# Last stage: scores computed with tokens as rows, and the compression units of four tiles stacked in column groups

## The reference, cut to what matters

```
cluster_scores = xf @ cluster_sigs.T            # 8 columns
tile_scores    = xf @ sigs.T                    # 64 columns
h    = gelu(xf @ compress_w1 + compress_b1)     # 32 units
comp = tanh(h @ compress_w2 + compress_b2)      # 2 values
```

## Time and profile before

| | |
|---|---|
| median of 3 runs | 1382.83 us (1378.61 to 1390.34) |
| the profiled execution | 1387.69 us, its span 1385.9 us |
| PE busy | 1106.9 us, 80% of the span |
| DVE busy | 1053.8 us, 76% |
| ACT busy | 834.5 us, 60% |
| POOL busy | 593.4 us, 43% |

### The profile page before, as it was taken

How to read it: one execution, slowest core, us unless ns; L and a number is a source line. 1 busy time by engine, 2 the same in 40 slices (tenths; PEclk the granted TensorE clock), 3 DMA queues, 4 the chain that set the end, 5 groups by cost and what they waited for, 6 DMA issues and landing times. The chain is left out here.

```text
span 1385.9 us, 36351 instructions
## 1 busy us (share of the span) xinstructions
PE 1106.9 (80%) x11411; PEld 781.1 (56%) x11411; DVE 1053.8 (76%) x2823; ACT 834.5 (60%) x1904; POOL 593.4 (43%) x696
## 2 busy tenths in 40 slices
PE   2599999999999997514999999999999997601330
PEld 1366666666666664303777777777777774301220
DVE  6478988998988894643777777777777772698885
ACT  1267777777777775362666676666666664401675
POOL 6224444344344432414554545555455505000676
PEclk9789999999999999756999999999999998855555
DMA  1645555555555540305544444444445421100011
GB/s 41 154 107 138 132 128 136 127 129 139 128 134 131 135 111 6 122 8 138 126 114 114 119 117 122 117 107 126 112 121 120 107 53 69 54 0 0 24 46 53
DMA packets 122515, 137.28 MB, mean 99 GB/s; under 512 B 12560, under 2 KB 110160, under 8 KB 113232
## 3 DMA queue, kind: packets, MB, share of 16 engines
q1 hardware_dynamic: 121408, 136.45, 39.7%
q10 hardware_dynamic: 1040, 0.00, 0.0%
HBM read 85.03 MB, written 37.75 MB: 89 GB/s over the span
## 5 line engine op out<-in xcount | busy, mean ns | idle before, releaser
L372 DVE TENSOR_REDUCE attn_negmax<-attn_row_ps 128x2 f32<-128x512 f32 (+1 forms) x1024 | 610.7, 618 | 204.4 <-PE attn_row_ps L554 186.1
L313 ACT ACTIVATE attn_probs<-attn_col_ps 128x512 f32<-128x512 f32 (+1 forms) x1024 | 541.3, 550 | 248.0 <-PE attn_col_ps L576 246.2
L554 PE MATMUL attn_row_ps<-k_st,q_st 72*128 72x256 bf16 (+1 forms) x2048 | 370.8, 263 | 15.7 <-DMA k_st<-attn_scratch 14.0
L576 PE MATMUL attn_col_ps<-q_st,k_st 74*128 74x256 bf16 (+1 forms) x2048 | 370.2, 262 | 1.6 <-ACT attn_probs L313 0.7
L593 PE MATMUL attn_out_ps<-attn_probs,v_sb 128*32 128x256 f32 (+1 forms) x4096 | 242.8, 361 | 0.7 <-ACT attn_probs L313 0.7
L576 PEld LDWEIGHTS attn_col_ps<-q_st,k_st 74*128 74x128 bf16 x2048 | 184.1, 99 | 89.6 <-ACT attn_probs L313 57.2
L554 PEld LDWEIGHTS attn_row_ps<-k_st,q_st 72*128 72x128 bf16 x2048 | 202.1, 99 | 42.2 <-issue 15.5
L593 PEld LDWEIGHTS attn_out_ps<-attn_probs,v_sb 128*32 128x32 f32 x4096 | 109.3, 110 | 90.1 <-issue 29.0
L287 POOL TENSOR_SCALAR attn_var<-attn_mv 128x2 f32<-128x2 f32 x64 | 14.3, 223 | 329.6 <-DVE attn_mv L435 329.6
L550 PE MATMUL attn_row_ps<-mask_qk,ident_h 128*128 128x256 bf16 x512 | 140.8, 275 | 18.0 <-DMA k_st<-attn_scratch 17.5
L572 PE MATMUL attn_col_ps<-mask_kq,ident_h 128*128 128x256 bf16 x512 | 141.5, 276 | 0.6 <-ACT attn_probs L313 0.5
(11 more groups left out here) (230 smaller groups left out, 1707.4 us busy)
## 6 DMA issues: line engine op xcount, KB each, us to landing
q_st<-attn_scratch SPq DMA_DIRECT2D x192, 192.0 KB
k_st<-attn_scratch SPq DMA_DIRECT2D x192, 192.0 KB
attn_scratch<-attn_parts SPq DMA_DIRECT2D x64, 384.0 KB, 2.8
attn_scratch<-attn_parts SPq DMA_DIRECT2D x64, 128.0 KB, 2.8
x_in<-in_L_attn_x_dram SPq DMA_DIRECT2D x32, 128.0 KB, 2.6
x_all<-in_L_attn_x_dram SPq DMA_DIRECT2D x32, 128.0 KB, 6.9
moe_xs<-x_all SPq DMA_DIRECT2D x8, 512.0 KB, 3.5
x_in<-x_mid SPq DMA_DIRECT2D x32, 128.0 KB, 2.5
```

What stands on the lines that cost most here:

```text
L313: nc.scalar.activation(probs_of(st, 3, u)[:, j, 0:W], col_ps[:, n % 2, 0:W], ACT.Exp, scale=scale).then_inc(probs_kept, 1)
L372: nc.vector.tensor_reduce(negmax[:, t, 2 * p:2 * p + 2], row_ps[:, row_bank(st, u), 0:2 * keys].rearrange("p (a k) -> p a k", a=2), AX_X, ...
L554: last = nc.tensor.matmul(bank[:, a * keys:(a + 1) * keys], q_st[0:KROWS, sl, h, t * P:(t + 1) * P], k_st[0:KROWS, sl, h, 0:keys], start=n ...
L576: last = nc.tensor.matmul(bank[:, t * N:(t + 1) * N - first], k_st[0:rows, sl, h, t * P:(t + 1) * P], q_st[0:rows, sl, h, first:N], start= ...
```

## The change

**On PE**, the one product with tokens as columns is replaced by two sets:

- units: four products per group, stationary `compress_w1` (128 x 32), moving the `xT` of tile t (128 columns), each written to rows 32t to 32t+31 of `h_ps`, so in four column groups of the array;
- scores: four products per group, stationary the `xT` of tile t (128 x 128), moving the 72 signature columns. The result has tokens as rows, so the back transposes (L1298, L1300) and the copy to `sT` (L1364) go.

**The second product** becomes one: the stationary is `hT`, now 128 rows (4 tiles x 32 units) by 128 tokens, the moving one a block-diagonal `cw2` (128 x 8). It yields two values for each tile, tokens as rows. The copy to `compT` (L1326) goes. Gelu works on 128 x 128 instead of 32 x 512.

**The pipeline** is one step shorter (depth 4 instead of 5). **The loads**: the bias and `compress_w2` are each loaded four times, once for each block of 32 rows, so that 25 transfers are issued instead of 19.

```diff
-SPLINE_LOADS = 9 + 2 * 5
+SPLINE_LOADS = 7 + 2 * SG + 2 * 5
...
+    for t in range(SG):
+        rows = slice(COMP * t, COMP * (t + 1))
+        eng.dma_start(cb1[rows, :], w["L1_ffn_compress_b1"].rearrange("(n one) -> n one", one=1))\
+            .then_inc(mem["ffn_loaded"], 16)
+        eng.dma_start(cw2[rows, 2 * t:2 * t + 2], w["L1_ffn_compress_w2"]).then_inc(mem["ffn_loaded"], 16)
...
-            pipeline(eng, step, 2, 5, SPLINE_GROUPS, 0)
+            pipeline(eng, step, 2, 4, SPLINE_GROUPS, 0)
...  (PE)
                         wait(pe, h_kept, st.seq(2))
-                        wait(pe, sT_kept, st.seq(2))
-                        nc.tensor.matmul(p_ps[:, j, :], sigs[:, :], xT[:, j, :], start=True, stop=True)\
-                            .then_inc(products_ready, 1)
+                        for t in range(SG):
+                            last = nc.tensor.matmul(h_ps[COMP * t:COMP * (t + 1), j, 0:P], sigs[:, AT_H:P],
+                                                    xT[:, j, t * P:(t + 1) * P], start=True, stop=True,
+                                                    skip_group_check=True)
+                        last.then_inc(h_ready, 1)
+
+                        wait(pe, scores_kept, st.seq(2))
+                        for t in range(SG):
+                            last = nc.tensor.matmul(s_ps[:, j, t * NS:(t + 1) * NS], xT[:, j, t * P:(t + 1) * P],
+                                                    sigs[:, 0:NS], start=True, stop=True)
+                        last.then_inc(scores_ready, 1)
                     if st.has(2):
                         j = st.slot(2)
                         pe.wait_ge(h_kept, st.seq(2, c=1))
-                        wait(pe, compT_kept, st.seq(3))
-                        apart(pe, mem)
-                        for t in range(SG):
-                            last = nc.tensor.matmul(c_ps[32 * t:32 * t + 32, j, 0:P], cw2[AT_H:P, :],
-                                                    hT[AT_H:P, j, t * P:(t + 1) * P], start=True, stop=True,
-                                                    tile_position=(AT_H, 32 * t), skip_group_check=True)
-                        last.then_inc(compT_ready, 1)
-                    if st.has(3):
-                        j = st.slot(3)
-                        pe.wait_ge(sT_kept, st.seq(3, c=1))
-                        pe.wait_ge(compT_kept, st.seq(3, c=1))
-                        wait(pe, scores_kept, st.seq(4, 2))
-                        for t in range(SG):
-                            nc.tensor.transpose(s_ps[:, j, t * NS:(t + 1) * NS], sT[:, j, t * P:(t + 1) * P],
-                                                ident[0:NS, 0:NS])
-                        nc.tensor.transpose(s_ps[:, j, COMP_AT:COMP_AT + P], compT[:, j, :], ident[:, :])\
-                            .then_inc(scores_ready, 1)
+                        wait(pe, hidden_kept, st.seq(3))
+                        nc.tensor.matmul(c_ps[:, j, 0:2 * SG], hT[:, j, :], cw2[:, :], start=True, stop=True)\
+                            .then_inc(hidden_ready, 1)
...  (ACT)
-                        nc.scalar.activation(hT[AT_H:P, j, :], p_ps[AT_H:P, j, :], ACT.Gelu, bias=cb1[AT_H:P, :])\
+                        nc.scalar.activation(hT[:, j, :], h_ps[:, j, 0:P], ACT.Gelu, bias=cb1[:, :])\
...
-                        nc.scalar.copy(compT[:, j, :], c_ps[:, j, 0:P]).then_inc(compT_kept, 1)
...  (DVE)
+                    if st.has(1):
+                        j, tiles = st.slot(1), bass.ds(st.seq(1, SG), SG)
+                        dve.wait_ge(scores_ready, st.seq(1, c=1))
                         nc.vector.tensor_copy(scores[:, tiles, :].rearrange("p t n -> p (t n)"),
+                                              s_ps[:, j, 0:SG * NS]).then_inc(scores_kept, 1)
+                    if st.has(2):
+                        j, tiles = st.slot(2), bass.ds(st.seq(2, SG), SG)
+                        dve.wait_ge(hidden_ready, st.seq(2, c=1))
+                        nc.vector.tensor_copy(comp[:, tiles, :], c_ps[:, j, 0:2 * SG].rearrange(
+                            "p (t m) -> p t m", m=2)).then_inc(hidden_kept, 1)
-                        nc.vector.tensor_copy(sT[:, j, :], p_ps[0:NS, j, :]).then_inc(sT_kept, 1)
```

More of the change, by code:

```diff
@@ L1110, in load_spline @@
                    (sigs[:, AT_H:P], w["L1_ffn_compress_w1"]),
-                   (cb1[AT_H:P, :], w["L1_ffn_compress_b1"].rearrange("(n one) -> n one", one=1)),
-                   (cw2[AT_H:P, 0:2], w["L1_ffn_compress_w2"]),
                    (mem["cb2"][:, :], wide(w["L1_ffn_compress_b2"], 2)),
@@ L1186, in spline_ffn @@
         xT = sb("xT", [P, 2, SG * P])
-        sT = sb("sT", [NS, 2, SG * P])
-        hT = sb("hT", [P, 2, SG * P])
-        compT = sb("compT", [P, 2, P])
+        hT = sb("hT", [P, 2, P])
         scores = sb("scores", [P, TILES, NS])
@@ L1212, in spline_ffn @@
         xs_loaded = [sem(f"xs_loaded{j}") for j in range(2)]
[L1213 to L1216, removed]
+        xT_ready, xT_kept, h_ready, h_kept = (sem(x) for x in ("xT_ready", "xT_kept", "h_ready", "h_kept"))
+        scores_ready, scores_kept, hidden_ready, hidden_kept = (
+            sem(x) for x in ("scores_ready", "scores_kept", "hidden_ready", "hidden_kept"))
         x_beta_kept, mv_cleared = sem("x_beta_kept"), sem("mv_cleared")
@@ L1222, in scored @@
         def scored(eng, step):
-            pipeline(eng, step, 2, 5, SPLINE_GROUPS, 0)
+            pipeline(eng, step, 2, 4, SPLINE_GROUPS, 0)
         with nc.psum_tensor("ffn_t_ps", [P, 2, 512], F32) as t_ps, \
-                nc.psum_tensor("ffn_p_ps", [P, 2, 512], F32) as p_ps, \
+                nc.psum_tensor("ffn_h_ps", [P, 2, 512], F32) as h_ps, \
                 nc.psum_tensor("ffn_c_ps", [P, 2, 512], F32) as c_ps, \
                 nc.psum_tensor("ffn_s_ps", [P, 2, 512], F32) as s_ps, nc.Block() as block:
-            COMP_AT = SG * NS
             @block.sync
@@ L1310, in step @@
                         act.wait_ge(xT_ready, st.seq(0, c=1))
-                        wait(act, products_ready, st.seq(1))
+                        wait(act, scores_ready, st.seq(1))
                         nc.scalar.copy(xT[:, j, :], t_ps[:, j, :]).then_inc(xT_kept, 1)
@@ L1315, in step @@
                         j = st.slot(1)
-                        act.wait_ge(products_ready, st.seq(1, c=1))
-                        wait(act, compT_ready, st.seq(2))
-                        nc.scalar.activation(hT[AT_H:P, j, :], p_ps[AT_H:P, j, :], ACT.Gelu, bias=cb1[AT_H:P, :])\
+                        act.wait_ge(h_ready, st.seq(1, c=1))
+                        wait(act, hidden_ready, st.seq(2))
+                        nc.scalar.activation(hT[:, j, :], h_ps[:, j, 0:P], ACT.Gelu, bias=cb1[:, :])\
                             .then_inc(h_kept, 1)
[L1321 to L1325, removed]
-                        nc.scalar.copy(compT[:, j, :], c_ps[:, j, 0:P]).then_inc(compT_kept, 1)
                 scored(act, step)
@@ L1351, in step @@
                 def step(st):
-                    if st.has(3):
-                        j, tiles = st.slot(3), bass.ds(st.seq(3, SG), SG)
-                        dve.wait_ge(scores_ready, st.seq(3, c=1))
+                    if st.has(1):
+                        j, tiles = st.slot(1), bass.ds(st.seq(1, SG), SG)
+                        dve.wait_ge(scores_ready, st.seq(1, c=1))
                         nc.vector.tensor_copy(scores[:, tiles, :].rearrange("p t n -> p (t n)"),
[L1356 to L1363, removed]
-                        nc.vector.tensor_copy(sT[:, j, :], p_ps[0:NS, j, :]).then_inc(sT_kept, 1)
+                                              s_ps[:, j, 0:SG * NS]).then_inc(scores_kept, 1)
[4 more added lines that the diff above has]
+                            "p (t m) -> p t m", m=2)).then_inc(hidden_kept, 1)
                 scored(dve, step)
-                dve.wait_ge(scores_kept, 2 * SPLINE_GROUPS)
+                dve.wait_ge(scores_kept, SPLINE_GROUPS)
+                dve.wait_ge(hidden_kept, SPLINE_GROUPS)
                 nc.vector.tensor_tensor(comp[:, :, :], comp[:, :, :], cb2[:, :].unsqueeze(1).broadcast_to([P, TILES, 2]),
@@ L1811, in build @@
                 "cb1": sb("cb1", [P, 1]),
-                "cw2": sb("cw2", [P, 32]),
+                "cw2": sb("cw2", [P, 2 * SG]),
                 "cb2": sb("cb2", [P, 2]),
```

## The result

| | median | runs | |
|---|---|---|---|
| before | 1386.28 us | 4 (1378.61 to 1390.34) | with one more run than was shown ahead of the prediction |
| changed | 1408.63 us | 4 (1404.74 to 1412.32) | ratio 1.0167, 95% interval 1.0132 to 1.0203 |

The change makes the kernel 1.7% slower, about 22 us; the whole interval lies above 1. I had forecast 1379.5 us and "same", with 0.05 on slower.

The account below looks back on a forecast made before the run. PE was taken to bound the serial scoring phase; head +0.23, middle -1.34 and tail -2.20 sum to -3.3 us, from the runs' median of 1382.83 to a forecast of 1379.5 us, range 1370 to 1388.

Parts of the forecast that it names:

- What bounds the kernel, and that the phase is serial: Scoring phase, 37.8 us: PE sets the pace, and what PE saves there comes off the end of the run.
- The period: One steady group of the scoring phase on PE: 2.03 us after the change against 2.16 before, 0.13 less.
- The lower and the upper bound: Price of one score pass on PE: 0.075 as in the back transposes, 0.168 if load and product don't overlap; 0.108 taken.
- The Trainium skill's rule on loads: Score passes on PE: loads using all rows would not overlap a running product, 0.168 a pass; rival at 1387.3, chance 0.10.
- Column groups without a tile position: Unit products on PE: four run side by side, 0.21 instead of 0.86; rival one by one at 1390, chance 0.04.
- Costed at nothing: Gelu, ACT's and DVE's copies and six more weight transfers: hidden in the other engines' slack, no time gained or lost.
- Head: Start of the scoring phase on PE: clock changes at about 1167.05, third group starts 0.23 us later.
- the clock falls: Rival for the scoring phase: granted clock drops to its lower level, +24 us in all, 1407; chance 0.03.
- the size of the sum: Whole run: head, middle and tail of the scoring phase, +0.23 - 1.34 - 2.20 = -3.3 us.

Follow-up runs that it names:

- e2_prewarm: The changed kernel with five unread f32 products of 256 columns on PE ahead of the first group; 1377.81 us, ratio 0.9978.
- e1: The changed kernel with score products moving all 128 columns of the signature matrix instead of 72; 1381.29 us, ratio 0.9988.
- e5: The changed kernel with five unread 256-column products before the first group and score products of all 128 columns; 1382.25 us, ratio 0.9983.
- e6: The kernel before with five unread f32 products of 256 columns ahead of its scoring phase; 1382.78 us, ratio 0.9985.
- e12: The changed kernel with one unread 256-column product ahead of the first group; 1403.22 us, ratio 1.0128.
- e8: The changed kernel with five early unread products, PE held in its fourth step until GpSimd's twelfth addition; 1408.09 us, ratio 1.0164.
- e9: The changed kernel with five early unread products, 128-column score products and PE held in its fourth step; 1387.40 us, ratio 1.0022.

## Why the prediction was wrong

- **What bounds the kernel, and that the phase is serial**: right. The phase grew by 22.85 us and the median by 22.35.
- **The period**: the sum holds at the clock for which it was worked out. By the starts in e2_prewarm the transposes take 0.56, the units 0.36, the scores 0.95 and the second product 0.19, in all 2.06 against 2.03 (0.60, 0.35, 0.86, 0.22). The scores were 0.09 too cheap, which the transposes and the second product mostly make up by chance. A pass of the scores is spaced by its load, as I took from a load with 1 column at half speed: eight loads of 0.192 in 0.97, spaced 0.111 against my 0.108.

```profile
1171.17 0.97 PEld L1284 LDWEIGHTS ffn_s_ps<-sigs,ffn_xT 128*128 128x128 f32 x8 [0.20 <-issue]
```

In the fast clock 56 more columns cost nothing (2.06 in e1 as well). The lower and the upper bound, 0.075 and 0.168 for a pass, were both unneeded.
- **The Trainium skill's rule on loads.** The Trainium skill ("TensorE: Matmul & The Clock Gate", Part 3, "The mechanism") would have loads of all rows wait for the running product; the same section also names a background weight buffer, whose loads are pulled ahead, which the prediction left out. If they waited, a pass of e1 would take its load and its 128 columns one after the other, 0.108 + 0.107, and a group an estimated 2.9 us. A group of e1 takes 2.06. The measurement decides: load and product overlap here.
- **Column groups without a tile position**: they run side by side (eight passes in 0.36, where one by one they would take 0.86), as taken.
- **Costed at nothing**: right. The six more transfers moved SP's last issue from 19.11 to 21.90, and DVE began the tables at 24.86 (24.88 before).
- **Head**: the failed step, and with it the clock of 1.00 that every term behind it assumes. That "the clock changes at about 1167.05", 3.6 us after the first transposes, was read from the kernel before and carried over, as if the rise came with time. Before, PE went from the transposes into two passes of 512 columns; after, into the unit products and eight full loads with 72 columns each. There it never rose: 0.50 for all 60.66 us, 3.76 us a group instead of 2.03. I used a rise of the old work for the new work. (The addition in this step ends at 1167.32, not 1167.35, which changes nothing.)
- **The rival "the clock falls"** had the right price, +24 us and 1407, and looked at the right thing, few columns beside many loads, but had a chance of 0.03. It was put as a fall from a clock already up, and argued away by a stretch at 1150 in which PE, busy for 3 of 5 us, kept 1.00. That row tells about holding. It says nothing of rising from 0.50, which is the state in which the phase begins, as the earlier trace rows show too (0.50 at 1166). e2 shows that on holding the argument was even right.

So the size of the sum was not at fault: with the clock up, the change gives 2.1 us (e1, whose first 5.3 us are slow) to 3.5 us (e5 against e6) of phase, for a forecast of 3.3. What failed was the condition under which it was made. Why the clock follows the mix of instructions in this way no run shows; they show only with which mixes it rose.

## What to carry to other kernels

Where PE enters a phase with the clock at 0.50, ask of the new instruction mix whether it raises the clock, and apart from it whether it holds it; rows at 1.00 answer the second question only. Here the same group held 1.00 for 29 us (e2) and stayed at 0.50 for 60 us (changed). Products that replace a wide moving operand by many full f32 weight loads with few columns behind each leave PE "busy" in the profile and may leave it at half speed: read the clock column beside the busy column. Where the load sets the pace of a pass, moving more columns behind it cost nothing here at 1.00 (2.06 us a group with 72 and with 128), and it made the phase 24.9 us shorter.

## What the runs showed of the hardware that was not expected

- The granted clock has memory: the same group of instructions ran at 1.00 from its first product to the last (e2) and at 0.50 from its first to its last (changed, e12, and e8 after its stop), depending on the level at which it began. In e8 13 groups in a row stayed at 0.50, 51 us of PE without a gap.
- A stop of PE of 5.5 us costs these 5.5 us and 2.3 more with the 128-column form, which is slow for one group (phase 46.3 in e9, 38.5 in e5), and 5.5 and some 24 more with the 72-column form (68.2 in e8, 38.7 in e2).
- Entering and leaving products in column groups leaves the weight loader idle each time: 0.33 us ahead of the unit products and 0.38 ahead of the score products at 0.50 (changed), 0.17 and 0.20 at 1.00 (e2).
